# Three buffers for the split spectrum, its matmuls moved behind the first band, and a new order of work on VectorE

## The reference, cut to what matters

```python
x = x + layer(_gn(x), W_in, W_dw, fft_weight, W_out)      # twice
# _gn: mean and variance of every channel of every image, 32 groups of one channel
xm = einsum('bchw,oc->bohw', x, W_in)                      # 3 x 85 channels
x_spatial, x_freq, x_gate = split(xm, 3, axis=1)
out_spatial = depthwise 3x3 convolution of x_spatial
xf = rfft2(8x8 patches of x_freq) * fft_weight
out_freq = irfft2(xf)
x_fused = gelu(x_gate) * (out_spatial + out_freq)
return einsum('bchw,oc->bohw', x_fused, W_out)
```

## Time and profile before

| what | value |
|---|---|
| median of 3 runs | 773.0 us (770.43 to 773.76) |
| the profiled execution, its own time | 775.2 us |
| span of its instructions | 773.4 us |
| mean granted TensorE clock | 0.985 of full speed |
| TensorE matmuls busy | 723.6 us, 94% |
| VectorE, ScalarE, GpSimd busy | 545.1, 572.5, 624.1 us |
| share of TensorE in the chain that ended last | 72% |

### The profile page before, as it was taken

One profiled execution on the slowest core, in us unless ns is written; L12 is line 12 of the kernel. 1 busy time (PEld: TensorE's weight loads), 2 busy tenths in 40 slices (PEclk: granted clock), 3 DMA queues, 4 the chain that ended last, 5 costly groups with the idle time before them and its releaser, 6 DMA issues.

```text
span 773.4 us, 32267 instructions
## 1 busy us (share of the span) xinstructions
PE 723.6 (94%) x12324; PEld 620.0 (80%) x12324; DVE 545.1 (70%) x957; ACT 572.5 (74%) x1087; POOL 624.1 (81%) x1071
## 2 busy tenths in 40 slices
PE   2589989999999999999999999999999999999997
PEld 1477778877888878888788888889888988898875
DVE  7578867878877876777777687666666676667543
ACT  1676667777787778878887778787778777877754
POOL 1977777888888898888888987988788888988871
PEclk9689999999999999999999999999999999999999
DMA  8676888787767765677766766877767777787741
GB/s 299 162 182 174 195 181 211 170 190 174 180 177 191 182 160 152 163 167 182 189 171 165 166 183 176 216 190 199 190 176 192 194 199 204 194 209 191 191 129 56
DMA packets 96259, 140.61 MB, mean 182 GB/s; under 512 B 32498, under 2 KB 34746, under 8 KB 95978
## 3 DMA queue, kind: packets, MB, share of 16 engines
q1 hardware_dynamic: 64390, 103.30, 51.6%
q0 software_dynamic: 25376, 26.75, 14.1%
q10 hardware_dynamic: 6340, 8.49, 4.3%
HBM read 10.81 MB, written 8.54 MB: 25 GB/s over the span
## 4 chain that ended last, share of the span: by engine, by line
PE 72%; DVE 7%; issue 6%; POOL 6%; DMA 5%; ACT 2%; SPq 1%; ACTq 0%; POOLq 0%; DVEq 0%
PE ps_s L543 29%; PE ps_ft L594 12%; PE ps_o L616 7%; PE ps_g L549 5%; DMA xs<-xf 4%; PE ps_z L639 4%; PE ps_s L656 4%; PE ps_s L654 4%; PE ps_xt L511 3%; POOL xs L425 2%; PE ps_x L523 2%; PE ps_x L524 2%; POOL yl L844 1%; DVE y L1120 1%; POOL stack L305 1%
## 5 line engine op out<-in xcount | busy, mean ns | idle before, releaser
L543 PE MATMUL ps_s<-cw,stack 128*128 128x85 f16 (+1 forms) x7168 | 407.3, 203 | 1.8 <-DMA stack<-parts 1.6
L425 POOL DMA_DIRECT2D xs<-xf x757 | 385.2, 513 | 15.7 <-PE ps_z L639 12.5
L543 PEld LDWEIGHTS ps_s<-cw,stack 128*128 128x128 f16 (+1 forms) x7168 | 352.8, 99 | 27.4 <-issue 1.9
L844 POOL TENSOR_TENSOR yl<-y,yh 128x340 f16<-128x340 f32 x256 | 219.0, 856 | 105.2 <-ACT yh L777 103.1
L1120 DVE TENSOR_TENSOR y<-ps_z,weff 128x340 f32<-128x340 f32 x256 | 129.6, 506 | 136.8 <-PE ps_z L639 129.9
L777 ACT ACTIVATE yh<-y 128x340 f16<-128x340 f32 x256 | 124.6, 487 | 135.2 <-DVE y L1120 118.1
L1029 DVE TENSOR_TENSOR parts<-xn,parts 128x1024 f16<-128x1024 f32 (+2 forms) x99 | 126.9, 1284 | 63.8 <-ACT parts L707 63.5
L594 PE MATMUL ps_ft<-squares_sb,g 128*85 128x128 f32 x1024 | 163.4, 282 | 0.8 <-ACT turned_results L765 0.8
L765 ACT ACTIVATE turned_results<-ps_ft 85x512 f32<-85x512 f32 x256 | 149.3, 583 | 16.7 <-issue 10.0
L770 ACT ACTIVATE g<-ps_g,gsc 128x340 f32<-128x340 f32 x256 | 137.2, 536 | 18.7 <-PE ps_g L549 18.2
L1097 DVE TENSOR_TENSOR g<-ps_s,g 128x340 f32<-128x340 f32 x256 | 128.2, 501 | 11.0 <-PE ps_s L656 8.1
(11 more groups left out here) (108 smaller groups left out, 548.0 us busy)
## 6 DMA issues: line engine op xcount, KB each, us to landing
stack<-parts SPq DMA_DIRECT2D x496, 130.0 KB, 3.6
xs<-xf POOLq DMA_DIRECT2D x757, 32.0 KB, 2.8
out_y<-yo SPq DMA_DIRECT2D x16, 512.0 KB, 3.1
stack<-parts SPq DMA_DIRECT2D x93, 64.5 KB, 2.9
stack<-parts SPq DMA_DIRECT2D x93, 64.0 KB, 2.8
x<-in_x SPq DMA_DIRECT2D x16, 256.0 KB, 6.0
stack<-parts ACTq DMA_DIRECT2D x62, 65.0 KB, 3.8
stack<-parts SPq DMA_DIRECT2D x62, 65.0 KB, 2.8
```

The costliest lines, as they stand in the source:

```text
L425: eng.dma_start(xs[C * k:C * k + C, h % HELD, q, :], xf[C * q:C * q + C, h % 2, SPECTRA[k], :]).then_inc(loaded, 16)
L543: mm(ps_s[i % 2][:, HID * q:HID * (q + 1)], pixels(kind, i, q, dy, rows), w[0:rows, m, :], start=(q == 0 and m == 0), stop=False)
L844: nc.gpsimd.tensor_tensor(yl[:, k, :], y32[:, k, :], yh[:, k, :], ALU.subtract).then_inc(s_yl, 1)
```

## The change

`yh` and `yl` get a third buffer (`YS = 3`), indexed by tile modulo 3; their waits for `s_s` are for tile i-1 instead of tile i. To make room, `out_edge` becomes the memory of `same`, with a wait for the second join before its first use, and seven one-column tensors become slices of one tensor `columns`. On TensorE the block of z of tile i+2 moves from behind the conv of band 3 to right behind the conv of band 0, ahead of the transposes. On VectorE `lo_of_spectrum` moves ahead of g, and y of tile i+2 moves ahead of the split parts. ScalarE's and GpSimd's orders stay.

```diff
+YS = 3
-        out_edge = sb("out_edge", [128, H])
+        out_edge = same
-        yh = sb("yh", [128, 2, GC], F16)
-        yl = sb("yl", [128, 2, GC], F16)
+        yh = sb("yh", [128, YS, GC], F16)
+        yl = sb("yl", [128, YS, GC], F16)
@@ tensor
                     conv_begins(i)
                     conv(i, 0)
+                if live(i, 2):
...
+                    if (i + 2) % GROUP == 0:
+                        spectra_loaded((i + 2) // GROUP)
+                    need(pe, s_y, i + 2)
...
+                    z.then_inc(s_z, 1)
                 if live(i, -2):
...
                     conv(i, 2)
                     conv(i, 3)
-                if live(i, 2):
...
-                    z.then_inc(s_z, 1)
...
-                    s, k = ps_s[i % 2], i % 2
+                    s, k = ps_s[i % 2], i % YS
@@ scalar
                     need(act, s_y, i + 3)
-                    need(act, s_s, i + 1)
-                    nc.scalar.activation(yh[:, i % 2, :], y32[:, i % 2, :], ACT.Copy).then_inc(s_yh, 1)
+                    need(act, s_s, i + 3 - YS)
+                    nc.scalar.activation(yh[:, (i + 2) % YS, :], y32[:, i % 2, :], ACT.Copy).then_inc(s_yh, 1)
@@ gpsimd
                 pool.wait_ge(s_res, (strip + 1) * TPS // OUT)
+                pool.wait_ge(s_joined, JOINED)
...
-                    k = i % 2
-                    need(pool, s_s, i + 1)
+                    k, k3 = i % 2, (i + 2) % YS
+                    need(pool, s_s, i + 3 - YS)
@@ vector
             for i in steps():
+                if i in leaving:
+                    lo_of_spectrum(leaving[i])
                 if live(i, -1):
...
                     v.tensor_tensor(g[:, k, :], ps_s[k][:, 0:GC], g[:, k, :], ALU.mult).then_inc(s_f, 1)
-                if i in leaving:
-                    lo_of_spectrum(leaving[i])
+                if live(i, 2):
...
+                                    ALU.mult).then_inc(s_y, 1)
                 def split_beside():
...
-                if live(i, 2):
...
-                                    ALU.mult).then_inc(s_y, 1)
```

More of the change, by code:

```diff
@@ L151, in build @@
         wo = [sb(f"wo{i}", [HID, C]) for i in range(LAYERS)]
-        gsc = [sb(f"gsc{i}", [128, 1]) for i in range(LAYERS)]
-        osc = [sb(f"osc{i}", [128, 1]) for i in range(LAYERS)]
+        columns = sb("columns", [128, 2 * LAYERS + 3])
+        gsc = [columns[:, i:i + 1] for i in range(LAYERS)]
+        osc = [columns[:, LAYERS + i:LAYERS + i + 1] for i in range(LAYERS)]
+        ve, power, table = (columns[:, 2 * LAYERS + i:2 * LAYERS + i + 1] for i in range(3))
         st = [sb(f"st{i}", [128, 2 * STRIPS, 6]) for i in range(LAYERS)]
@@ L159, in build @@
         mv = sb("mv", [128, len(STATS), 2])
-        ve = sb("ve", [128, 1])
-        power = sb("power", [128, 1])
         nr = sb("nr", [128, 3])
@@ L164, in build @@
         rstd_edge = sb("rstd_edge", [128, len(STATS), 2])
-        table = sb("table", [128, 1])
         xt = sb("xt", [128, PAIR, 2, 128], F16)
@@ L588, in _ @@
                     conv(i, 0)
+                if live(i, 2):
+                    if (i + 2) % LT == 0:
+                        pe.wait_ge(s_projection, PROJECTIONS * (layer(i + 2) + 1))
+                        pe.wait_ge(s_weff, layer(i + 2) + 1)
+                    if (i + 2) % GROUP == 0:
+                        spectra_loaded((i + 2) // GROUP)
+                    need(pe, s_y, i + 2)
+                    col = 128 * ((i + 2) % GROUP)
+                    for q in range(Q):
+                        z = mm(ps_z[:, HID * q:HID * (q + 1)], xs[:, (i + 2) // GROUP % HELD, q, col:col + 128],
+                               pw[layer(i + 2)][0:3 * C, 0, :], start=(q == 0), stop=(q == Q - 1))
+                    z.then_inc(s_z, 1)
                 if live(i, -2):
@@ L840, in _ @@
                 if live(i, 2):
-                    k = i % 2
-                    need(pool, s_s, i + 1)
+                    k, k3 = i % 2, (i + 2) % YS
+                    need(pool, s_s, i + 3 - YS)
                     need(pool, s_yh, i + 3)
-                    nc.gpsimd.tensor_tensor(yl[:, k, :], y32[:, k, :], yh[:, k, :], ALU.subtract).then_inc(s_yl, 1)
+                    nc.gpsimd.tensor_tensor(yl[:, k3, :], y32[:, k, :], yh[:, k3, :], ALU.subtract).then_inc(s_yl, 1)
                 for e, at in AGGREGATING.items():
@@ L1097, in _ @@
                     v.tensor_tensor(g[:, k, :], ps_s[k][:, 0:GC], g[:, k, :], ALU.mult).then_inc(s_f, 1)
-                if i in leaving:
-                    lo_of_spectrum(leaving[i])
+                if live(i, 2):
+                    k = i % 2
+                    need(dve, s_z, i + 3)
+                    need(dve, s_yl, i + 1)
+                    v.tensor_tensor(y32[:, k, :].rearrange("p (q o) -> p q o", q=Q),
+                                    ps_z[:, 0:GC].rearrange("p (q o) -> p q o", q=Q),
+                                    weff[layer(i + 2)][:, None, :].broadcast_to([128, Q, HID]),
+                                    ALU.mult).then_inc(s_y, 1)
                 def split_beside():
```

## The result

The changed kernel takes 840.9 us (median; 834.3 to 849.0), against 772.7 us before: the ratio is 1.086, with a 95% interval of 1.079 to 1.093. The direction was the forecast one, but the loss is 68 us where 27 were forecast, outside the range of 768 to 820. Medians are of all executions and ratios of the faster ones; two experiments (yh ahead of the gelu, filler) were profiled in a slower execution, so their traces give waits and clocks and no totals.

The account below looks back on a forecast made before the run. TensorE was taken as the bound: 49.6 us of new z waits against 27.1 us won, +3 for GpSimd and +2 outside the stretch, made +27 on 775.2, 802; 800 us for the median, range 768 to 820.

Parts of the forecast that it names:

- The bound and its waits: TensorE, busy 94% of the span, bounds the kernel; 27.1 us of its waits lie in steps 14 to 242.
- the transform's waits: TensorE, steps 0 modulo 4: waiting for the low part of the spectrum, 0.25 us in step 204, would go.
- z in front comes ahead of its data: Steps 2 modulo 4: moved z would wait for its group's last DMA, 0.87 us per group, 49.6 us in all.
- the rivals: Spectra land in time, 747 us, chance 0.12; both cancel, 773, 0.08; VectorE becomes the wait, 769 to 811, 0.05.
- VectorE's wait: Third rival: y or parts late on VectorE, z or conv waiting 0.7 to 2 us per strip; chance 0.05.
- the sum: Steps 14 to 242: 49.6 us of new z waits against 27.1 us of old waits, giving +22.5 us.
- the floor of 618.5: TensorE, steps 14 to 242: 57 groups of four steps without waits, 10.85 us each.
- The formula: Steps 2 modulo 4: z waits the landing time of the group's last DMA minus 2.35 us, once per group.
- T: End of step 203 on TensorE, 625.35 us; the group's last DMA was forecast to start at T + 2.63.
- the five: Five sampled landings of a group's last DMA, 2.4 to 4.3 us, giving a mean z wait of 0.87 us.
- +2 us: Loss allowed for the groups outside steps 14 to 242: the first three and the last two.
- GpSimd's stalls: GpSimd held up in 7 DMA issues, 12.5 us in all; a quarter, +3 us, was booked.

Follow-up runs that it names:

- filler: The changed kernel with 44 matmuls on a constant ahead of TensorE's wait for the DMAs in ten steps: 840.1 us, ratio 1.084.

## Why the prediction was right in kind and wrong in size

**What held.** The bound and its waits; the transform's waits go; z in front comes ahead of its data; the data follow yl, yl yh, and yh the gelu; yl ends at 1.6 us where 1.69 was worked out. A wait of z near 50 to 60 us in 40 to 60 times was forecast, and 74.2 us in 50 times were measured (56.4 us in 44 times from step 14 to step 242). VectorE's wait for z, forecast to shrink by more than half, shrank by 46%. None of the rivals took part: VectorE's wait did not come, since y stands ahead of the parts.

**What failed, in order of size.** From step 14 to step 242 the sum had +22.5 us. The last matmuls of these two steps in the changed kernel, in the timeline of PE:

```profile
96.27 0.31 PE L659 MATMUL ps_s<-yl,waves 128*128 128x340 f16 x1
...
797.41 0.49 PE L659 MATMUL ps_s<-yl,waves 128*128 128x340 f16 x1
```

That is 701.1 us to the starts, against 645.6: +55.5. Above the floor of 618.5 the stretch has 82.6 us of waits and slow steps. They are TensorE's idle time, 56.4 us, all of it z's wait for DMAs; 8 us for the 0.17 us by which each such wait costs more; and 18 us of slow steps.

1. *No term for the clock.* The sum took the time behind a wait as unchanged: "TensorE's number of matmuls is the same, so the floor of 10.85 us stays". The slow tails in the stretch (8 of the 10, and the starts of the steps behind) are 18 us of the 82.6. This put the clock at nothing without a reason. The trace of before had such a case: TensorE stood idle for 1.95 us ahead of z of group 6 in step 22, and the window behind it, which is for the most part step 23, is at 0.72.

```profile
113.20:117.00 3.80, 3.80 (x52) 3.64 (x51) 2.71 (x5) 2.55 (x6) 2.66 (x4) 0.72 0.12 30
```

2. *The wait was mis-sized.* 82.6 - 18 = 65 us over 57 groups is 1.14 us a group, where 0.87 was taken: 15 us. The formula was right: with each group's own issue (2.66 us behind T on average, 2.63 was forecast) and own landing (3.39 us on average, 3.22 in the five) it gives 1.10. What failed was the sample. The trace of before shows the landing of a group's last DMA for 20 groups, 2.1 to 6.2 us; the formula makes 1.08 us a group of all 20 and 0.87 of the five that were taken, in which no landing was over 4.3 us. In the changed kernel the groups 6, 8, 10, 11, 13, 39, 45 and 61 waited 2.4 to 4.1 us, with late landings or a DMA issue that was held up. The row's maximum of 6.2 us was in sight and stood in no bound.
3. *The start.* Step 14 ends at 96.58 against 87.43, 9 us late, from waits of z of 3.7 and 3.9 us in steps 6 and 14 with slow tails after both. In step 14 the last DMA took 6.7 us to land, the longest of all. In the kernel before, the same DMA took 6.2 us and had landed 0.2 us ahead of z's start. Behind step 242 another 2 us were lost. For all this together +2 us was put down.

Together 18 + 15 + 9 + 2 = 44 us, less the +2 for outside the stretch and the +3 for GpSimd's stalls, which are in the measured waits: 39 us. The span grew by 67 us where 27 were forecast, 40 more.

**What is no failure of the prediction.** It booked 0.65 us for an early z, an early y and the third buffer together, and 0.74 was measured. Only my later expectation that the third buffer gives nothing fell: without it the change is at 863.7.

## What to carry to other kernels

Before a matmul that reads a DMA's landing is moved forward in TensorE's order, the slack from landing to first use must be read for each such place, the long landings with the median; here 1.3 us stood against a move of 2.6. Where the landings scatter, the mean of the waits is what counts, and a few long landings carry it: take all that the trace has. An instruction at the end of a producer's in-order queue moves up only as far as the one ahead of it lets it. When the bound engine gets new waits, its clock is a term of its own, and what helped was to move the issue of the DMAs, not the use: one step earlier was worth 79 us with z in front (840.9 to 762.1) and 10 us with z in its old place (769.3 to 759.3).

## What the runs showed of the hardware

A wait of TensorE of 1.5 us (in step 38 of the run with two buffers) was once followed by half clock, and one of 2.7 us (step 50 of the changed kernel) was not. A fall costs from 1.3 to 2.7 us in a step of 3.5, so 50 waits of which ten end so are 21 us dearer than their length. The landings of line 428 in the changed kernel ranged from 1.6 to 6.7 us with a median of 2.6, all of 32 KB; the last DMA of a group of twelve took 3.4 us on average. GpSimd stood idle for 1.0 to 2.4 us ahead of seven single DMAs of this line in the kernel before and in the changed one, ahead of the same seven of the 757; no run shows why.
